# Expert rows of a mixture-of-experts block regrouped: 32 pair tiles of 2 x 48 rows become 24 tiles of 128 rows, with a merge product and eight gathers ahead

## The chip, the cores and the metric

The kernel runs on one core of one Trainium2 chip. The metric is the device time of that core in microseconds, lower is better. The kernel before took 1391.23 us (median of 3 runs).

## What is computed

The block is one transformer layer in float32 over 16 sequences of 256 tokens with 256 features (4096 tokens). Its first part is a decayed linear attention with 32 heads, then a residual and a layer norm without gains; the result is called x1. Its second part, which the change is about, is a mixture of experts on x1, then a residual and a layer norm again:

```python
scores = sigmoid(x @ gate_w)                       # 64 experts, 8 groups, the best 4 groups
topk_ids = top_k(masked scores + bias, 6)          # 6 experts a token
topk_w = scores[topk_ids] / sum * 2.5
order = argsort(flat expert of every (token, k))
pos = place within its expert
tok = order // K                                   # K = 6
valid = pos < CAP                                  # CAP = 2*(256*6//64) = 48
buf[expert, pos] = x[tok]                          # 64 experts x 48 rows of 256
h = silu(buf @ w_gate) * (buf @ w_up)              # 256 -> 96
out = h @ w_down                                   # 96 -> 256
y = segment_sum(out * topk_w, tok)                 # added to the token's row
y += silu(x @ ws_gate) * (x @ ws_up) @ ws_down     # shared expert, all tokens
```

So each of the 64 experts handles at most 48 rows, 3072 rows in all, and one token can stand under several experts.

## The kernel before, in words

The kernel is written by hand, engine by engine, with semaphores. Each engine runs its own program in order; SP issues the plain DMAs, POOL the indirect ones.

**Attention, us 0 to about 1200.** A loop over 16 sequences and 8 head groups (`sequences`, `step` on each engine). The router of the sequence before, the search for the tokens of each expert (`search`, `slots_*`) and the stores of x1 run in between. x1 with the 64 routing weights of each token behind it goes to `gather_rows` (4096 rows of 320 floats, 1280 bytes). The output sums lie in `sums`, two regions of 4096 rows of 256 floats.

**Tail of the attention, about 1200 to 1230.** No projections are left, and TensorE works on the shared expert, cut into 16 units (one of each sequence): `unit_gate_up` (g), `unit_down` (d), in the order of `TAIL`. Twelve units (`UNITS_AHEAD`) are done here; their elementwise products are POOL's (`unit_product`, L1486), the last of them before POOL's first gather. When the tokens of all experts are known (`ids`, 64 experts x 48), VectorE lays them out (L1381 to L1387), TensorE turns them into one column for each pair by a small product (L729 to L732), and VectorE writes the indices for the gathers and the slot numbers (L1389, L1390). Experts are taken in **pairs**: pair p has expert 2p in rows 0 to 47 and expert 2p+1 in rows 64 to 111 (`BANDS` = 112, `BAND` = 64; rows 48 to 63 stay unused). A scatter with addition must not hold the same row twice, so `find_doubles` (L1392 to L1403) compares the token numbers of both halves: SP writes them to memory (L473) and reads them back, broadcast (L475), and VectorE compares (L1396), reduces (L1398) and replaces the place of a doubled row (L1401, L1403).

**Loop over 32 pairs, about 1233 to 1336.** The order on TensorE in iteration p is written out (L791 to L803): `keep_busy` (L740, a product of 512 columns that nothing reads) and the two transposes of pair p+1 (`transpose_tokens`, L750), `gate_up(p)` (L761: 4 products of 192 columns, into partitions 0 to 47 and 64 to 111), `transpose_inner(p-1)` (L768, and L771, which puts the doubled rows of the second expert under the first's), `down(p-2)` (L778: 3 products of 256 columns). ScalarE evacuates the transposes (L1009), takes the SiLU (L1014) and evacuates the inner transpose (L1019). VectorE multiplies SiLU, weight and up-projection (L1419, two halves of 48 rows) and evacuates the result (`wo`, L1411, 4 buffers). In iterations 2, 8, 14 and 20 (`UP_AT`), and two later (`DOWN_AT`), TensorE also does one of the four units left.

POOL gathers 6 pairs ahead (`AHEAD`, 8 buffers), and for each pair p issues first gather p+6 (L1519), then scatter p (L1525). The scatter waits for `wo(p)`, and for the landing of scatter p-2:

```python
def scatter(p):
    pool.wait_ge(s_wo, p + 1)
    wait(pool, s_sc[p % 2], 16 * (p // 2))
```

SP loads the expert weights (576 KB for a pair, L454 and L455) into a ring of 16 pairs. The first 12 are loaded before the loop, and then one for each pair that is done:

```python
for p in range(FIRST_PAIRS, PAIRS):
    sp.wait_ge(s_md, p - FIRST_PAIRS + 1)
    load_pair(p, p % RING)
```

**End, about 1342 to 1385.** When all scatters have landed, SP reads both regions of `sums` in 16 pieces (L486), and VectorE, POOL and ScalarE add them, take the layer norm and store.

Of the kernel before, what the change touches and what calls it, by code (L numbers as in the profile page):

```python
# [15 lines left out]
F32 = mybir.dt.float32  # L16
F16 = mybir.dt.float16
U32 = mybir.dt.uint32
# [22 lines left out]
BANDS = 112  # L41
BAND = 64
# [5 lines left out]
AHEAD = 6  # L48
# [61 lines left out]
def block_kernel(nc, x, xT, wprep, normw, decay, eye, tri, w_router, bias2, w_shared, w_shared_down,  # L110
                 w_experts, w_down, slot_consts, dummy_rows, out):
# [9 lines left out]
    ids_t = nc.dram_tensor("slot_ids", (PAIRS, 2, CAP), F32, kind="Internal").ap()  # L121
# [3 lines left out]
    with ExitStack() as ctx:  # L125
# [3 lines left out]
        def sem(name):  # L129
# [86 lines left out]
        ids = sb("ids", [EXP, BAND])  # L216
        idsg = sb("idsg", [EXP, BAND])
        idss = sb("idss", [EXP, BAND])
        slotf = sb("slotf", [BANDS, PAIRS])
        twice = sb("twice", [BANDS, PAIRS])  # L220
        first = sb("first", [EXP, 1])
        slotc = sb("slotc", [EXP, 3 + PAIRS + BAND])
        dummies = sb("dummies", [P, PAIRS])
        pick, pairof, region, dummy = (slotc[:, 0:2], slotc[:, 2:2 + PAIRS], slotc[:, 2 + PAIRS:3 + PAIRS],
                                       slotc[:, 3 + PAIRS:3 + PAIRS + BAND])
        bandg = sb("bandg", [EXP, BANDS])
        bands = sb("bands", [EXP, BANDS])
        gidx = sb("gidx", [BANDS, PAIRS], U32)
        sidx = sb("sidx", [BANDS, PAIRS], U32)
# [9 lines left out]
        xg = carve(BANDS, XRING, ROW)  # L239
        wo = carve(BANDS, OUTBUF, HID)  # L240
        xgT = carve(P, 2, NC * BANDS).rearrange("p s (c n) -> p s c n", c=NC)
        mhs, mh, mhT = carve(BANDS, 2, FF), carve(BANDS, 2, FF), carve(FF, 2, BANDS + CAP)
# [21 lines left out]
        S1 = S[:, :, :].rearrange("p h n -> p (h n)")  # L264
        same = S1[0:BANDS, 0:PAIRS * CAP].rearrange("p (k n) -> p k n", k=PAIRS)

# [5 lines left out]
        pT, pH, pHT, pDn = [pA, pS[:, 0, :]], [pB, pS[:, 1, :]], [pC, pC], [pS[:, 2, :], pS[:, 3, :]]  # L272
# [55 lines left out]
        s_ring = [sem(f"s_ring{i}") for i in range(RING)]  # L328
# [6 lines left out]
        s_idr, s_idb, s_same, s_twice = sem("s_idr"), sem("s_idb"), sem("s_same"), sem("s_twice")  # L335
        s_sidx = sem("s_sidx")
# [12 lines left out]
        UP_AT = {2 + 6 * i: UNITS_AHEAD + i for i in range(SEQS - UNITS_AHEAD)}  # L349
# [33 lines left out]
        def _(sp):  # L383
# [10 lines left out]
            for i in range(PARTS):  # L394
# [8 lines left out]
                     (wsh, w_shared), (wsd[:, :], w_shared_down), (slotc[:, :], slot_consts), (dummies[:, :], dummy_rows)]  # L403
# [49 lines left out]
            def load_pair(p, r):  # L453
                sp.dma_start(ring[r][:, 0:4 * NC * FF], w_experts[p]).then_inc(s_ring[r], 16)  # L454
                sp.dma_start(ring[r][0:FF, 4 * NC * FF:PAIR_W], w_down[p]).then_inc(s_ring[r], 16)  # L455
# [27 lines left out]
            for i in range(2):  # L483
                sp.wait_ge(s_sc[i], 16 * (PAIRS // 2))
# [6 lines left out]
        def _(pe):  # L491
# [238 lines left out]
            for dst, a in ((pC, bandg), (pO, bands)):  # L730
                last = nc.tensor.matmul(dst[0:BANDS, 0:PAIRS], a[:, :], pairof, start=True, stop=True)
# [873 lines left out]
```

## Time and profile before

| | |
|---|---|
| median of 3 runs | 1391.23 us (1386.91 to 1393.55) |
| the profiled execution's own time | 1386.84 us |
| its span | 1385.0 us |
| busy TensorE | 1317.2 us (95%) |
| busy VectorE, ScalarE, POOL | 1178.0, 951.9, 457.1 us |
| attention and tail, to the first transpose of the pair loop | 0 to 1233.5 us |
| pair loop | 1233.5 to 1336.0 us |
| last scatter | issued at 1338.65, landed at about 1342.3 us |
| sums read, normed and stored | 1342.4 to 1385 us |

The time of the profiled execution is 1.84 us more than its span, which is what lies around the span. It stands 0.3% under the median and at the fast end of the three runs. Times in the rows below count from the start of the span.

### The profile page before, as it was taken

To read this page: it belongs to the slowest core of one execution; us is meant where nothing else is said; L and a number is where in the kernel's file an instruction comes from. 1 tells how busy PE (TensorE), PEld (TensorE's weight loads), DVE (VectorE), ACT (ScalarE), POOL (GpSimd) and SP (SyncE) were. 2 spreads that over 40 slices of the span, in tenths; PEclk is the share of its full clock that TensorE was granted. 3 is DMA by queue.
4 is the path that set the end of the run, shared out by engine and by line. 5 is a ranking of instruction groups with operands and counts; after the bars stand their busy time and mean duration, and the time that the engine had idled before them with its cause. 6 is when DMAs were issued, how large, how long until landed. Compare 5 with 4: busy or idle time off the path is not lost.

```text
span 1385.0 us, 39168 instructions
## 1 busy us (share of the span) xinstructions
PE 1317.2 (95%) x14971; PEld 1093.4 (79%) x14971; DVE 1178.0 (85%) x2393; ACT 951.9 (69%) x1735; POOL 457.1 (33%) x310
## 2 busy tenths in 40 slices
PE   7999999999999999999999999999999999889950
PEld 5888888888888888888888888888888888765530
DVE  7989899898989898999899898989898989653337
ACT  7777777777777777777777777777777777533315
POOL 0222322332323223232323233323223232447754
PEclk9999999999999999999999999999999999999985
DMA  8500000000000010100000000000010100879857
GB/s 315 203 2 17 27 17 26 17 27 17 26 17 26 9 34 1 38 5 17 26 17 26 17 26 17 26 17 26 9 34 9 34 1 22 270 233 257 220 117 298
DMA packets 53061, 88.00 MB, mean 64 GB/s; under 512 B 6752, under 2 KB 32192, under 8 KB 52032
## 3 DMA queue, kind: packets, MB, share of 16 engines
q1 hardware_dynamic: 41728, 70.33, 15.2%
q0 software_dynamic: 5632, 8.26, 3.4%
q10 hardware_dynamic: 5568, 7.34, 1.5%
q8 instruction: 119, 1.95, 0.6%
q14 instruction: 14, 0.11, 0.0%
HBM read 60.08 MB, written 25.83 MB: 62 GB/s over the span
## 4 chain that ended last, share of the span: by engine, by line
PE 89%; DMA 5%; DVE 2%; issue 2%; ACT 1%; POOL 1%; SPq 0%; ACTq 0%; DVEq 0%; POOLq 0%
PE pA L495 25%; PE pB L495 25%; PE pO L592 12%; PE pC L579 10%; PE pS L557 10%; DMA sums<-sb_stage,sb_sidx 2%; PE pC L495 2%; PE pS L778 1%; DMA sb_stage<-gather_rows,sb_gidx 1%; DMA sb_W<-sums 1%; PE pB L761 1%; PE pC L614 1%; PE pS L761 1%; PE pS L495 0%; SPq L486 0%
## 5 line engine op out<-in xcount | busy, mean ns | idle before, releaser
L1479 POOL TENSOR_TENSOR sb_acc<-sb_acc,sb_sq 128x512 f32<-128x512 f32 x112 | 246.1, 2197 | 681.8 <-ACT sb_sq L879 681.8
L495 PE MATMUL pB<-sb_xh,sb_W 128*128 128x256 f16 x2048 | 351.3, 274 | 0.5 <-ACT sb_kh L842 0.5
L495 PE MATMUL pB<-sb_xl,sb_W 128*128 128x256 f16 x1024 | 279.7, 273 | 0.0
L1095 DVE TENSOR_TENSOR sb_S<-pS,sb_D 128x1024 f32<-128x1024 f32 x250 | 231.6, 949 | 36.1 <-PE pS L557 35.4
L1101 DVE TENSOR_TENSOR sb_Shl<-sb_S,sb_Shl 128x1536 f16<-128x1536 f32 x122 | 220.1, 1804 | 2.3 <-ACT sb_Shl L868 2.0
L495 PEld LDWEIGHTS pB<-sb_xh,sb_W 128*128 128x128 f16 x2048 | 192.9, 99 | 32.8 <-DVE sb_W L1053 1.3
L868 ACT ACTIVATE sb_Shl<-sb_S 128x1024 f16<-128x1024 f32 x244 | 192.3, 835 | 12.2 <-DVE sb_S L1095 2.3
L495 PE MATMUL pA<-sb_xh,sb_W 128*128 128x256 f16 x1024 | 175.8, 274 | 5.6 <-DVE sb_W L1053 5.6
L495 PE MATMUL pA<-sb_W,sb_xh 128*128 128x256 f16 x1024 | 176.0, 274 | 2.2 <-ACT sb_qh L835 2.2
L592 PE MATMUL pO<-sb_Wo,sb_yh 128*128 128x256 f16 x1024 | 174.7, 273 | 1.5 <-DVE sb_yl L1074 1.5
L1074 DVE TENSOR_TENSOR sb_yl<-sb_y,sb_yh 128x512 f16<-128x512 f32 x128 | 161.4, 1261 | 2.1 <-ACT sb_yh L884 2.1
L579 PE MATMUL pC<-sb_Shl,sb_vh 128*64 128x128 f16 (+1 forms) x1952 | 144.1, 249 | 0.6 <-DVE sb_Shl L1101 0.6
L841 ACT ACTIVATE sb_k<-pB 128x512 f32<-128x512 f32 x128 | 76.5, 597 | 95.6 <-PE pB L495 95.6
L495 PE MATMUL pA<-sb_xl,sb_W 128*128 128x256 f16 x512 | 140.2, 274 | 0.0
L592 PE MATMUL pO<-sb_Wo,sb_yl 128*128 128x256 f16 x512 | 139.6, 273 | 0.0
L495 PE MATMUL pA<-sb_W,sb_xl 128*128 128x256 f16 x512 | 139.6, 273 | 0.0
L834 ACT ACTIVATE sb_q<-pA 128x512 f32<-128x512 f32 x128 | 76.4, 597 | 84.7 <-PE pA L495 84.7
L557 PE MATMUL pS<-sb_qh,sb_kl 64*128 64x256 f16 (+1 forms) x1024 | 126.0, 243 | 0.0
L874 ACT ACTIVATE sb_gt<-pB 128x512 f32<-128x512 f32 x128 | 76.4, 597 | 68.4 <-PE pB L495 66.4
L579 PEld LDWEIGHTS pC<-sb_Shl,sb_vh 128*64 128x64 f16 x1952 | 102.2, 110 | 26.2 <-issue 25.4
L579 PE MATMUL pC<-sb_Shl,sb_vl 128*64 128x256 f16 x976 | 121.0, 246 | 0.0
L557 PE MATMUL pS<-sb_qh,sb_kh 64*128 64x256 f16 (+1 forms) x1024 | 120.7, 245 | 0.0
(223 smaller groups left out, 2698.4 us busy)
## 6 DMA issues: line engine op xcount, KB each, us to landing
sb_stage<-wprep SPq DMA_DIRECT2D x7, 1280.0 KB, 6.3
sb_W<-sums SPq DMA_DIRECT2D x16, 512.0 KB, 11.4
sb_W<-w_experts SPq DMA_DIRECT2D x16, 384.0 KB, 5.8
gather_rows<-sb_xr SPq DMA_DIRECT2D x16, 320.0 KB, 2.3
sb_D<-w_experts SPq DMA_DIRECT2D x12, 384.0 KB, 4.0
sb_xs<-xT SPq DMA_DIRECT2D x17, 256.0 KB, 2.9
sb_D<-decay SPq DMA_DIRECT2D x8, 512.0 KB, 7.3
sb_xn<-x SPq DMA_DIRECT2D x16, 256.0 KB, 3.0
```

Source lines behind the costliest of these rows:

```text
L495: last = nc.tensor.matmul(dst, a, m, start=(i == 0), stop=(i == len(terms) - 1), **kw)
L557: last = nc.tensor.matmul(pS[:, 2 * u + e, at:at + T - q0], k[lo:hi, u, k0:k0 + P], x_[lo:hi, u, q0:T], start=(n == 0), stop=(n == len(pro ...
L579: last = nc.tensor.matmul(pC[64 * e:64 * e + 64, u * T + t * P:(u + 1) * T], v[:, t, head * HD:(head + 1) * HD], s[:, head, a:z_], start=( ...
L592: last = nc.tensor.matmul(pO[:, t * HID:(t + 1) * HID], (yh, yl)[y][:, u * T + t * P:u * T + (t + 1) * P], Wo[:, w, q, u * HID:(u + 1) * H ...
L834: nc.scalar.activation(q32[:, :, :], bank, ACT.Silu, scale=1 / W_SCALE)
L841: nc.scalar.activation(k32[:, :, :], bank, ACT.Silu, scale=1 / W_SCALE)
L868: nc.scalar.activation(Sh[:, :, a:z_], S[:, :, a:z_], ACT.Copy).then_inc(s_Sh, 1)
L874: nc.scalar.activation(gt[q % 2][:, :], pB[:, :], ACT.Tanh, scale=0.5 / W_SCALE).then_inc(s_ge, 1)
L1074: nc.vector.tensor_tensor(yl[:, :], y32[:, :], yh[:, :], ALU.subtract).then_inc(s_yl, 1)
L1095: nc.vector.tensor_tensor(scores_at(h)[:, :, a:z_], pS[:, :, a:z_], d[:, :, 0:z_ - a], ALU.mult).then_inc(s_Sm, 1)
L1101: nc.vector.tensor_tensor(Sl[:, :, :], S[:, :, :], Sh[:, :, :], ALU.subtract).then_inc(s_Sl, 1)
L1479: nc.gpsimd.tensor_tensor(acc[:, :], acc[:, :], sq[:, :], ALU.add).then_inc(s_acc, 1)
```

## The change

The 48 slots of each expert are split into a main block of 32 rows (`BLOCK`) and a rest of 16 (`REST`). Eight experts fill three tiles of 128 rows: two tiles ("kinds" 0 and 1) hold the main blocks of four experts each, the third (kind 2) the rests of all eight. 64 experts make 24 tiles without gaps. For each block of 32 rows the product takes its own expert's weights and writes its own 32 output partitions; in a tile of kind 2 a block has rows of two experts, and its products run twice, with the other expert's 16 columns held at zero.

A token can stand in up to 4 (or 8) experts of one tile. `equal` (128 x 128) says which rows of a tile have the same token. It is multiplied with an upper triangle, and a last product (`merge`) adds to each row the rows of the same token before it; the rows that have a later one of the same token are sent to a dummy place, and only the last is scattered to the token. So the routing weight is applied before the merge, by ScalarE (`weighted`), and no longer in the product of SiLU and up-projection.

Eight gathers run ahead in place of six. The weight ring is released in groups of four pairs (three tiles). The last two products of the units ahead move from POOL to VectorE. The eight products that cleared the output banks (L788) go.

```diff
-    BANDS = 112
-    BAND = 64
+    TILES = EXP * CAP // P
+    KINDS = 3
+    BLOCK = 32
+    REST = CAP - BLOCK
-    AHEAD = 6
+    AHEAD = 8
+    EQS, EQB = 8, 4
+def experts_of(t):
+    g, kind = t // KINDS, t % KINDS
+    if kind < 2:
+        return [[8 * g + 4 * kind + j] for j in range(4)]
+    return [[8 * g + 2 * j, 8 * g + 2 * j + 1] for j in range(4)]
...
-        UP_AT = {2 + 6 * i: UNITS_AHEAD + i for i in range(SEQS - UNITS_AHEAD)}
+        UP_AT = {2 + 5 * i: UNITS_AHEAD + i for i in range(SEQS - UNITS_AHEAD)}
...
-            sp.dma_start(ids_t.rearrange("k e n -> (k e) n"), idss[:, 0:CAP]).then_inc(s_idr, 16)
-            sp.wait_ge(s_idr, 16)
-            sp.dma_start(same[BAND:BANDS, :, :], ids_t[:, 0, :].unsqueeze(0).broadcast_to([CAP, PAIRS, CAP])).then_inc(s_idb, 16)
+            sp.dma_start(ids_main, ids[:, 0:BLOCK]).then_inc(s_idr, 16)
+            sp.dma_start(ids_rest, ids[:, BLOCK:CAP]).then_inc(s_idr, 16)
+            sp.wait_ge(s_idr, 32)
+            n = EXP // 8 // 2
+            for i in range(2):
+                rows = id_rows[i].rearrange("p (g n) -> p g n", g=n)
+                for src, at, z_ in ((ids_main, 0, 2 * P), (ids_rest, 2 * P, KINDS * P)):
+                    src = src[i * EXP // 2:(i + 1) * EXP // 2, :].rearrange("(g e) n -> g (e n)", g=n)
+                    sp.dma_start(rows[:, :, at:z_], src.unsqueeze(0).broadcast_to([P, n, z_ - at])).then_inc(s_idb[i], 16)
             sp.wait_ge(s_D, STEPS)
             for p in range(FIRST_PAIRS, PAIRS):
-                sp.wait_ge(s_md, p - FIRST_PAIRS + 1)
+                sp.wait_ge(s_md, p - FIRST_PAIRS + 1 if p < RING else KINDS * ((p - RING) // 4 + 1))
                 load_pair(p, p % RING)
...
+            def gate_up(t):
+                blocks = experts_of(t)
+                pe.wait_ge(s_xgT, t + 1)
+                g = t // KINDS
+                pe.wait_ge(s_ring[g % (RING // 4)], 4 * 32 * (g // (RING // 4) + 1))
+                wait(pe, s_mh, t - 1)
+                parts = len(blocks[0])
+                for c in range(NC):
+                    for h in range(parts):
+                        for j, b in enumerate(blocks):
+                            at = slice(BLOCK * j, BLOCK * (j + 1))
+                            last = nc.tensor.matmul(pH[t % 2][at, 0:2 * FF], xgT[:, t % KINDS + h, c, at],
+                                                    ring_gu[b[h] // 2 % RING][:, b[h] % 2, c, :],
+                                                    start=(c == 0 and h == 0), stop=(c == NC - 1 and h == parts - 1))
                 last.then_inc(s_mgu, 1)
+            def transpose_inner(t):
+                pe.wait_ge(s_mh, t + 1)
+                wait(pe, s_mhT, t)
+                nc.tensor.transpose(pHT[0:FF, 0:P], mh[:, t % 2, :], ident[:, :]).then_inc(s_mht, 1)
+            def down(t):
+                pe.wait_ge(s_mhT, t + 1)
+                wait(pe, s_ysb, t)
+                for h in range(parts):
+                    for j, b in enumerate(blocks):
+                        at = slice(BLOCK * j, BLOCK * (j + 1))
+                        last = nc.tensor.matmul(pDn[at, 0:HID], mhT[t % KINDS + h][:, at], ring_d[b[h] // 2 % RING][:, b[h] % 2, :],
+                                                start=(h == 0), stop=(h == parts - 1))
                 last.then_inc(s_md, 1)
+            def merge(t):
+                pe.wait_ge(s_ysb, t + 1)
+                pe.wait_ge(s_eq, t + 1)
+                wait(pe, s_wo, t)
+                nc.tensor.matmul(pM[:, 0:HID], equal[t % EQS], ysb[t % 2], start=True, stop=True).then_inc(s_mm, 1)
...
-            for bank in pH + pDn:
-                nc.tensor.matmul(bank[0:BANDS, 0:HID], zeros[:, 0:BANDS], zeros[:, 0:HID], start=True, stop=True)
             transpose_tokens(0)
+            for p in range(TILES + 3):
+                if p + 1 < TILES:
                     transpose_tokens(p + 1)
+                if p < TILES:
                     gate_up(p)
+                if 1 <= p <= TILES:
                     transpose_inner(p - 1)
+                if 2 <= p <= TILES + 1:
                     down(p - 2)
+                if p >= 3:
+                    merge(p - 3)
...
+                if kind < 2:
+                    last = nc.scalar.activation(mhT[kind], pHT[0:FF, 0:P], ACT.Copy)
+                else:
+                    for h in range(2):
+                        to, at = [a.rearrange("p (j h n) -> p j h n", j=4, h=2)[:, :, h, :] for a in (mhT[kind + h], pHT[0:FF, 0:P])]
+                        last = nc.scalar.activation(to, at, ACT.Copy)
...
+            def weighted(t):
+                act.wait_ge(s_md, t + 1)
+                wait(act, s_mm, t - 1)
+                nc.scalar.activation(ysb[t % 2], pDn[:, 0:HID], ACT.Copy, scale=weight[:, t:t + 1]).then_inc(s_ysb, 1)
...
+            for dst, at, z_, n, pick in ((cand_main, 0, BLOCK, 4, pick_main), (cand_rest, BLOCK, CAP, 8, pick_rest)):
+                shape = [EXP, n, z_ - at]
+                last = nc.vector.tensor_tensor(dst[:, :].rearrange("e (l s) -> e l s", l=n), ids[:, at:z_].unsqueeze(1).broadcast_to(shape),
+                                               pick.unsqueeze(2).broadcast_to(shape), ALU.mult)
+            nc.vector.tensor_copy(slotf[:, :], pC[:, 0:TILES])
+            chain.link(nc.vector.tensor_scalar(gathf[:, :], pC[:, 0:TILES], float(TOK - 1), None, ALU.min))
+            chain.ready()
+            nc.vector.tensor_copy(gidx[:, :], gathf[:, :]).then_inc(s_idx, 1)
+            chain.link(nc.vector.tensor_tensor(slotr[:, :], slotf[:, :], region_less, ALU.add))
+            for j in (UNITS_AHEAD - 2, UNITS_AHEAD - 1):
+                unit_product(j)
+            def find_equals(n):
+                a, z_ = n * EQB, (n + 1) * EQB
+                dve.wait_ge(s_idb[a * P // half_rows], 32)
+                wait(dve, s_mm, z_ - EQS)
+                for t in range(a, z_):
+                    rows = id_rows[t * P // half_rows][:, t * P % half_rows:t * P % half_rows + P]
+                    nc.vector.scalar_tensor_tensor(equal[t % EQS], rows, slotf[:, t:t + 1], triu[:, 0:P], ALU.is_equal, ALU.mult,
+                                                   accum_out=count_eq[:, t:t + 1]).then_inc(s_eq, 1)
+                dve.wait_ge(s_eq, z_)
+                nc.vector.scalar_tensor_tensor(place[:, a:z_], count_eq[:, a:z_], FAR, slotr[:, a:z_], ALU.mult, ALU.add).then_inc(s_place, 1)
+                dve.wait_ge(s_place, 2 * n + 1)
+                nc.vector.tensor_tensor(placed[:, a:z_], place[:, a:z_], dummy[:, a:z_], ALU.min).then_inc(s_place, 1)
+                dve.wait_ge(s_place, 2 * n + 2)
+                nc.vector.tensor_copy(sidx[:, a:z_], placed[:, a:z_]).then_inc(s_sidx, 1)
+            find_equals(0)
+            def evacuate(t):
+                dve.wait_ge(s_mm, t + 1)
+                if t >= OUTBUF:
+                    dve.wait_ge(s_sc[t % 2], 16 * (t // 2 + 1 - OUTBUF // 2))
+                nc.vector.tensor_copy(wo[:, t % OUTBUF, :], pM[:, 0:HID]).then_inc(s_wo, 1)
+            for p in range(TILES + 3):
+                if p < TILES:
                     dve.wait_ge(s_mhs, p + 1)
                     wait(dve, s_mht, p - 1)
+                    nc.vector.scalar_tensor_tensor(weights8[:, p % 2, :], xg[:, p % XRING, at:at + 8], 1.0, onehot[:, p % KINDS, :],
+                                                   ALU.mult, ALU.mult, accum_out=weight[:, p:p + 1])
+                    nc.vector.tensor_tensor(mh[:, p % 2, :], mhs[:, p % 2, :], pH[p % 2][:, FF:2 * FF], ALU.mult).then_inc(s_mh, 1)
+                if p >= 3:
+                    evacuate(p - 3)
+                if p % EQB == EQB - 1 and p + 1 < TILES:
+                    find_equals(p // EQB + 1)
...
             def scatter(p):
+                pool.wait_ge(s_sidx, p // EQB + 1)
                 pool.wait_ge(s_wo, p + 1)
...
+            for p in range(TILES):
+                if p + AHEAD < TILES:
                     gather(p + AHEAD)
                 scatter(p)
```

## Rows read from the trace of the kernel before

**Rows 1.** The page: the span, and TensorE's busy time.
```profile
span 1385.0 us, 39168 instructions
...
PE 1317.2 (95%) x14971; PEld 1093.4 (79%) x14971; DVE 1178.0 (85%) x2393; ACT 951.9 (69%) x1735; POOL 457.1 (33%) x310
```

**Rows 2.** Windows: stretch, us, busy PE, PEld, DVE, ACT, POOL, clock, DMA, GB/s.
```profile
1237.00:1336.00 99.00, 97.79 (x689) 55.66 (x687) 35.04 (x101) 32.29 (x105) 69.22 (x57) 1.00 0.81 194
```

**Rows 3.** Timeline of TensorE, one iteration (start us, length us, instruction).
```profile
1254.85 0.39 PE L740 MATMUL pA<-sb_x1hl,sb_wshh 128*128 128x512 f16 x1
1255.08 0.36 PE L750 MATMUL pA<-sb_ident,sb_stage 112*128 112x112 f32 x2
1255.36 0.86 PE L761 MATMUL pS<-sb_W,sb_stage 128*48 128x192 f32 x8
1256.15 0.30 PE L768 MATMUL pC<-sb_ident,sb_stage 112*96 112x112 f32 x1
1256.38 0.36 PE L771 MATMUL pC<-sb_S,sb_stage 48*96 48x48 f32 x2
1256.68 1.06 PE L778 MATMUL pS<-sb_W,sb_stage 96*48 96x256 f32 x6
1257.67 0.39 PE L740 MATMUL pS<-sb_x1hl,sb_wshh 128*128 128x512 f16 x1
```

**Rows 4.** Timeline of TensorE: the down-projection of a unit, and what follows it.
```profile
1248.24 1.14 PE L495 MATMUL pO<-sb_wsd,sb_q 96*128 96x256 f32 x4
1249.21 0.38 PE L740 MATMUL pA<-sb_x1hl,sb_wshh 128*128 128x512 f16 x1
```

**Rows 5.** Timeline of TensorE from 1255.3 to 1255.6 us: instructions begun by then.
```profile
1255.36 0.53 PE L761 MATMUL pS<-sb_W,sb_stage 128*48 128x192 f32 x4
```

**Rows 6.** Timeline of TensorE: first and last row of a unit's gate and up.
```profile
1241.26 0.31 PE L495 MATMUL pO<-sb_W,sb_wshh 128*96 128x256 f16 x1
...
1242.60 0.38 PE L740 MATMUL pA<-sb_x1hl,sb_wshh 128*128 128x512 f16 x1
```

**Rows 7.** Timelines of VectorE, POOL, SP, TensorE at the loop's start; idle in brackets.
```profile
1233.32 1.75 DVE L1396 TENSOR_TENSOR sb_S<-sb_S,sb_slotf 48x1536 f32<-48x1536 f32 x1 [7.02 <-DMA sb_S<-slot_ids]
...
1229.09 1.19 POOL L1519 DMA_INDIRECT sb_stage<-gather_rows,sb_gidx  x1 [0.19 <-issue]
...
1228.76 0.35 SPq L475 DMA_DIRECT2D sb_S<-slot_ids  x1
...
1235.47 0.41 PE L750 MATMUL pS<-sb_ident,sb_stage 112*128 112x112 f32 x2 [1.32 <-DMA sb_stage<-gather_rows,sb_gidx]
...
1237.90 0.30 PE L768 MATMUL pC<-sb_ident,sb_stage 112*96 112x112 f32 x1
```

**Rows 8.** Timeline of POOL late in the loop: scatter, gather, scatter.
```profile
1313.00 1.49 POOL L1525 DMA_INDIRECT sums<-sb_stage,sb_sidx  x1 [0.30 <-issue]
1314.79 0.95 POOL L1519 DMA_INDIRECT sb_stage<-gather_rows,sb_gidx  x1 [0.30 <-issue]
1316.04 1.48 POOL L1525 DMA_INDIRECT sums<-sb_stage,sb_sidx  x1 [0.30 <-issue]
```

**Rows 9.** DMA queues and a scatter's landing, 1250 to 1275 us.
```profile
q1 hardware_dynamic: 1953, 4.53, 58.5%
q0 software_dynamic: 1287, 1.94, 41.3%
...
sums<-sb_stage,sb_sidx POOLq DMA_INDIRECT x8, 5.8
```

**Rows 10.** Groups of instructions and timeline of VectorE: evacuation; weighted copy with a sum.
```profile
L1411 DVE COPY sb_stage<-pS 112x256 f32<-112x256 f32 x32 | 13.6, 424 | 19.1 <-PE pS L778 19.1
...
1217.59 0.22 DVE L1212 SCALAR_TENSOR_TENSOR sb_wsel<-sb_mask,sb_sc 128x64 f32<-128x64 f16 x1
```

**Rows 11.** Timelines of TensorE and POOL: the last of the pair loop.
```profile
1334.11 1.93 PE L778 MATMUL pS<-sb_Wo,sb_stage 96*48 96x256 f32 x12
...
1338.65 1.45 POOL L1525 DMA_INDIRECT sums<-sb_stage,sb_sidx  x1 [0.63 <-issue]
```

More of the change, by code:

```diff
@@ L262, in block_kernel @@
         late_sh = [a.rearrange("p (k n) -> p k n", k=FIN) for a in late_sh]
-        S1 = S[:, :, :].rearrange("p h n -> p (h n)")
-        same = S1[0:BANDS, 0:PAIRS * CAP].rearrange("p (k n) -> p k n", k=PAIRS)
+        half_rows = TILES // 2 * P
+        id_rows = [a.rearrange("p h n -> p (h n)")[:, 0:half_rows] for a in (S[:, :, :], whole_S[1])]
         CHUNK = REGIONS * FIN * HID
@@ L327, in block_kernel @@
         s_slots = sem("s_slots")
-        s_ring = [sem(f"s_ring{i}") for i in range(RING)]
+        s_ring = [sem(f"s_ring{i}") for i in range(RING // 4)]
         s_gath = [sem(f"s_gath{i}") for i in range(XRING)]
@@ L334, in block_kernel @@
         s_sc = [sem(f"s_sc{i}") for i in range(2)]
[L335 to L336 removed]
+        s_idr, s_idb = sem("s_idr"), [sem(f"s_idb{i}") for i in range(2)]
+        s_eq, s_place, s_sidx = sem("s_eq"), sem("s_place"), sem("s_sidx")
+        s_ysb, s_mm = sem("s_ysb"), sem("s_mm")
         s_fl = [sem(f"s_fl{i}") for i in range(FINALS)]
@@ L729, in _ @@
             pe.wait_ge(s_ids, 1)
-            for dst, a in ((pC, bandg), (pO, bands)):
-                last = nc.tensor.matmul(dst[0:BANDS, 0:PAIRS], a[:, :], pairof, start=True, stop=True)
-            last.then_inc(s_idp, 1)
+            nc.tensor.matmul(pC[:, 0:TILES], cand_main[:, :], tile_main, start=True, stop=False)
+            nc.tensor.matmul(pC[:, 0:TILES], cand_rest[:, :], tile_rest, start=False, stop=True).then_inc(s_idp, 1)
             for u in "g11 d10 d11".split():
@@ new lines, in inner, with evacuate_inner @@
+            def inner(t):
+                act.wait_ge(s_mgu, t + 1)
+                wait(act, s_mh, t - 1)
+                nc.scalar.activation(mhs[:, t % 2, :], pH[t % 2][:, 0:FF], ACT.Silu).then_inc(s_mhs, 1)
+            def evacuate_inner(t):
+                act.wait_ge(s_mht, t + 1)
+                wait(act, s_md, t + 1 - KINDS)
+                kind = t % KINDS
+                if kind < 2:
+                    last = nc.scalar.activation(mhT[kind], pHT[0:FF, 0:P], ACT.Copy)
+                else:
+                    for h in range(2):
+                        to, at = [a.rearrange("p (j h n) -> p j h n", j=4, h=2)[:, :, h, :] for a in (mhT[kind + h], pHT[0:FF, 0:P])]
+                        last = nc.scalar.activation(to, at, ACT.Copy)
+                last.then_inc(s_mhT, 1)
@@ L1506, in step @@
                 if last_b and q == 3:
-                    for j in range(4, UNITS_AHEAD):
+                    for j in range(4, UNITS_AHEAD - 2):
                         unit_product(j)
@@ L1536, in _ @@
                 pool.wait_ge(done, 16 * len(range(i, UNITS_AHEAD, UEV)))
-            for p in range(PAIRS):
-                if p + AHEAD < PAIRS:
+            for p in range(TILES):
+                if p + AHEAD < TILES:
                     gather(p + AHEAD)
@@ L1595 @@
         "slot_consts": slot_consts,
-        "dummy_rows": (REGIONS * TOK + P * (pair % REGIONS)[None, :] + np.arange(P)[:, None]).astype(np.float32),
+        "row_consts": row_consts,
     }
```

194 lines of the change are left out of this document (73 added, 121 removed).

## The prediction

> **What bounds the kernel now.** I read the page first: TensorE is busy for 95% of the span [rows 1], but the change touches only the last 150 us, so its worth has to be read there. The windows view of the pair loop shows TensorE busy 97.8 of 99 us at the full granted clock, POOL 69 us, VectorE 35, ScalarE 32, and the DMA engines 81% [rows 2]. So the loop is bound by TensorE, with POOL and the DMAs not far behind. The timeline of TensorE splits one iteration into its groups; I take the step from the start of one group to the start of the next [rows 3]: idle filler 0.23, two transposes 0.28, gate and up 0.79, inner transpose 0.23, product for doubled rows 0.30, down 0.99; together 2.82 us. 32 pairs take 90.2 us. The four units in the loop take 1.34 us for gate and up [rows 6] and 0.97 for down [rows 4], 2.31 each, 9.2 in all. The sum, 99.4 us, stands against the 100.5 us from the transpose at 1235.47 [rows 7] to the last product's end at 1336.04 [rows 11]: the model holds.
>
> **Prices of matrix work.** The gate and up products are 8 instructions of 192 columns (a float32 product is two instructions). By 1255.6, 0.24 us after the first began, four had begun [rows 5]: two column groups run side by side, and 8 instructions are 4 rounds. A unit's down-projection runs its 4 instructions of 256 columns one after another: 0.97 us [rows 4]. L778 takes 0.99 for 6 instructions [rows 3]: two rounds of two and two of one, also 4 rounds. From 0.99 (4 rounds of 256) and 0.79 (4 rounds of 192, worth 3 of 256) a round of 256 costs 0.20, one of 192 costs 0.15, and each group has a head of 0.19.
>
> **The loop after the change, part by part.** The new products are in four blocks of 32 partitions. The trace shows two groups side by side, not four; I take it that four run as two do, since the second one costs nothing visible. One after another in twos is the other end, below.
> - Filler and transposes: 112 rows become 128, 0.23 + 0.31.
> - Gate and up, kinds 0 and 1: 8 products, 16 instructions, 4 rounds, 0.79. Kind 2: 32 instructions, 8 rounds, 0.19 + 1.20 = 1.39.
> - Inner transpose 0.24. The product L771 goes (0.30).
> - Down: kinds 0 and 1 two rounds, 0.59; kind 2 four rounds, 0.99.
> - Merge: one full product of 256 columns, two instructions: 0.19 + 0.40 = 0.59.
>
> So a tile of kind 0 or 1 takes 2.75 and one of kind 2 takes 3.75; three take 9.25, and 24 take 74.0 in place of 90.2. With the units' 9.2, unchanged, TensorE's loop is 83.2 us: **16.2 less**.
>
> **The start.** Before, POOL's first gather waits behind the last unit product and starts at 1229.09; TensorE's second transpose waits for the second gather until 1235.47, and VectorE stands 7.02 us until the slot numbers land at 1233.32, so that the first inner transpose starts only at 1237.90 [rows 7]. After: two products leave POOL's queue for VectorE's, which is idle there anyway; they delay only what stands behind them there, the equality, and it waits for a DMA. The first gather can go some 2 us earlier, an estimate that matters little, since the equality ends later than the gathers; and two gathers more cost POOL 2.5 us [rows 8] before its first scatter, at a time when it waits for the first result. The eight clearing products lie where TensorE waits for a gather: worth nothing. On VectorE the next thing late is the equality. The read-back grows from 0.29 to 1.57 MB (128 partitions x 3072 x 4 bytes) in four DMAs; the small one took 4.5 us from 1228.76 [rows 7]. It starts some 0.7 us earlier, and only its first half is needed first: I take the same landing, 1233, with 1232 and 1237 as ends. Then VectorE does 4 comparisons of 128 x 128 (two 64-wide instructions of the kind of 0.22 each with their reads of the sum [rows 10], 0.4) and three small steps, 2.4 us, until 1235.4; before, its work on the doubled rows lasted until shortly before 1237.90. With the first product of SiLU and up-projection, and the step to TensorE, the first inner product follows at 1236.4: **1.5 less**, from 2.5 less to 2.5 more.
>
> **VectorE and ScalarE in the loop.** VectorE: 0.3 weight, 0.3 product, 0.42 evacuation [rows 10], 0.6 for its share of comparisons: 1.6 us a tile. ScalarE gets a fourth evacuation, 1.3 to 1.7. Both lie under a tile's 2.75 to 3.75. But comparisons come in blocks of 2.4 us every fourth iteration, ahead of the next product in VectorE's queue. That product is wanted by TensorE one iteration later, after filler, transposes and gate-up; by my steps it is ready some 0.4 us before. I cost this at nothing; if a comparison takes 0.6 and not 0.4, five blocks lose about 0.4 us each, 2 us.
>
> **POOL and the DMAs.** One scatter and one gather with their gaps take 3.04 us [rows 8], almost all of 2.82. Rows go from 112 to 128: a scatter is 1.48 to 1.69 us, a gather 0.95 to 1.09, by a fixed cost or by rows. A tile is 3.03 to 3.38 us of POOL against TensorE's mean (83.2 / 24) of 3.47. So POOL stays just under. The DMAs: weights cost 58.5% of 25 us for 4.53 MB, 1.9 us of all engines a pair; tokens 41.3% of 25 us for 1.94 MB, 5.3 us a MB [rows 9]. Token traffic falls from 8.26 MB (32 x 112 rows of 1280 and 1024 bytes) to 7.08, but a tile is 0.295 MB, 1.6 us. The releases in groups of four bring all 20 pairs (38 us) into the first 13 tiles: 4.5 us of demand a tile against 3.47. The weights can be late, eight tiles lie between their issue and their use. The scatters cannot: scatter p waits for p-2. At 5.8 us [rows 9] and 0.8 to the next start, two scatters need 6.6 us before; with 128 rows 7.4, or 3.7 a tile over some 12 tiles, against 3.47: 2.8 us, most of it taken up by the four buffers. I put 2 us on the last scatter's distance behind TensorE.
>
> **The sum.** TensorE has done 2.97 us of its 83.2 before the first inner transpose (three pairs of transposes, two fillers, two gate-ups), so it ends at 1236.4 + 80.2 = 1316.6. The last scatter stood 2.6 us behind the end at 1336.04 [rows 11]; now 4.6, with 0.5 for its size: 1321.7 in place of 1338.65, **17 us less**. What follows is unchanged. On the profiled execution's 1386.84 that is 1369.8. It lies 4.4 us under the median, so the forecast for the median is 1391.23 - 17 = **1374**.
>
> **Rivals.**
> - **Two blocks at a time (slower).** If only two column groups run together, gate and up take 16 rounds of 0.15 more for three tiles and down 8 of 0.20: 4.0 us, 32 in all. TensorE ends at 1348.6, the last scatter at 1351.7: 13 us more, **1404**. It decides where a round of four costs more than 1.5 rounds of two (17 of 32). Against it: the second group started with no visible delay [rows 5]. For it: no row shows four, nor four streams of float32 read at once. Chance 0.12.
> - **Four blocks at a loss.** With rounds of four a quarter dearer, 24 rounds for three tiles (16 x 0.15 + 8 x 0.20 = 4.0) cost 1.0 more, 8 in all: **1382**. Chance 0.10. The Trainium skill ("TensorE: Matmul & The Clock Gate", Part 3, Packing small matmuls) gives 2.38 times for three column tiles of 32, that is 0.79 of the ideal; by that rule it would be this case, and the trace, whose two groups lose almost nothing, doesn't bear it out.
> - **Scatters set the pace.** With all weights pressed into the first 13 tiles a scatter takes 8.5 us to land (5.8 now): 4.6 us a tile to tile 14, from a first scatter at 1244 (1236.4 and two iterations and a unit's gate-up on) to 1309, then 2.5 a tile as the weights are in: 1331. The gain shrinks to 8: **1383**. For it: the DMA engines are full in that stretch already. Against: token packets and weight packets share them now and the lag stays small. Chance 0.10.
> - **A late read-back** of 1.57 MB shifts all by 3 or 4 us: **1378**. Chance 0.08, inside the range.
>
> **How the numbers follow.** The base case, with its own spread 1366 to 1380, has 0.56; the late read-back 0.08; the two at 1382 and 1383 have 0.20; two at a time 0.12; 0.04 for other things. The range 1364 to 1390 leaves out the slow rival and both tails, 0.2. A measurement of this kernel can tell about 0.5%, 7 us, from no change: faster than 1384.3 gets 0.77 (base, read-back, two thirds of the middle cases), within 0.5% 0.11, slower than 1398 0.12.
>
> **What the changed profile would show.** Timeline of a kind 0 tile: L761's successor with 16 instructions in about 0.8 us, the merge 0.6, three tiles in 9.3 us. The loop would end at about 1317 and the last scatter start near 1321. A gate and up of 1.4 us in kinds 0 and 1 would be the first rival; idle TensorE before merges or gathers with scatters over 8 us the third; a first comparison later than 1235 the fourth.

## The result: 0.6% faster

The changed kernel takes 1378.21 us (median of 5 runs, 1376.7 to 1383.0), the kernel before 1390.62 (5 runs). The ratio is 0.9939, with a 95% interval of 0.9916 to 0.9963: 8.5 us less, where 17 were forecast. The two medians lie 12.4 us apart, a little outside that interval. The five runs of the kernel before spread over nearly 8 us, and its three later sets of 17 runs have medians of 1386.6 to 1387.8, which is nearer to the ratio; so the text goes by ratios. The time lies within the forecast's range. The profiled executions took 1380.61 and 1386.84 us.

The page of the changed kernel:

```profile
span 1378.8 us, 39739 instructions
...
PE 1305.0 (95%) x15235; PEld 1085.5 (79%) x15235; DVE 1168.2 (85%) x2455; ACT 956.6 (69%) x1751; POOL 439.3 (32%) x292
...
q0 software_dynamic: 4608, 7.08, 2.6%
```

The packing does on TensorE what it was to do. A whole iteration with kind 0 or 1 (columns as in [rows 3]):

```profile
1243.76 0.38 PE L770 MATMUL pA<-sb_x1hl,sb_wshh 128*128 128x512 f16 x1
1243.98 0.38 PE L780 MATMUL pA<-sb_ident,sb_stage 128*128 128x128 f32 x2
1244.29 0.86 PE L794 MATMUL pS<-sb_W,sb_stage 128*32 128x192 f32 x16
1245.08 0.31 PE L802 MATMUL pC<-sb_ident,sb_stage 128*96 128x128 f32 x1
1245.32 0.64 PE L812 MATMUL pS<-sb_W,sb_qh 96*32 96x256 f32 x8
1245.89 0.70 PE L820 MATMUL pS<-sb_ql,sb_kh 128*128 128x256 f32 x2
1246.43 0.38 PE L770 MATMUL pS<-sb_x1hl,sb_wshh 128*128 128x512 f16 x1
```

Its gate and up has 16 instructions (L794) where [rows 3] has 8, in the same 0.79 us, and eight of them have begun by 1244.5, where [rows 5] had four:

```profile
1244.29 0.53 PE L794 MATMUL pS<-sb_W,sb_stage 128*32 128x192 f32 x8
```

Four blocks of 32 columns run as two of 48 did. The loop as a whole does not keep that pace. Windows of the changed kernel (columns: stretch, length, busy PE, PEld, DVE, ACT, POOL, clock, DMA share, GB/s):

```profile
1232.00:1240.00 8.00, 4.96 (x41) 2.35 (x41) 2.12 (x15) 1.58 (x7) 2.96 (x4) 0.57 0.84 307
1240.00:1272.00 32.00, 32.00 (x395) 19.18 (x396) 10.65 (x62) 15.03 (x50) 16.04 (x13) 1.00 0.84 224
1272.00:1284.00 12.00, 9.12 (x73) 5.10 (x66) 3.12 (x19) 2.40 (x8) 5.71 (x5) 0.72 1.07 291
1284.00:1294.00 10.00, 10.00 (x121) 5.74 (x119) 2.29 (x12) 5.11 (x17) 5.16 (x4) 1.00 1.01 299
1294.00:1304.00 10.00, 8.04 (x70) 3.85 (x72) 2.77 (x16) 1.91 (x7) 6.62 (x5) 0.67 0.76 192
1304.00:1326.00 22.00, 22.00 (x265) 12.40 (x261) 7.26 (x40) 9.96 (x34) 14.19 (x11) 0.99 0.46 66
```

There are three holes in TensorE's work, at 1232, 1274 and 1294 us, each with a clock under 1.00 behind it (the granted clock as a share of the full one; 0.50 is its lower level). The timeline of TensorE says what ended them (idle before the instruction in brackets):

```profile
1235.04 0.69 PE L780 MATMUL pS<-sb_ident,sb_stage 128*128 128x128 f32 x2 [3.11 <-DMA sb_stage<-gather_rows,sb_gidx]
...
1277.30 0.69 PE L780 MATMUL pS<-sb_ident,sb_stage 128*128 128x128 f32 x2 [2.88 <-DMA sb_stage<-gather_rows,sb_gidx]
...
1296.34 0.44 PE L780 MATMUL pS<-sb_ident,sb_stage 128*128 128x128 f32 x2 [1.96 <-DMA sb_stage<-gather_rows,sb_gidx]
```

All three wait for gathered rows. The chain of waits leads from there to scatters that take 9 to 10 us to land, against a median of 5.8 [rows 9], and to a gather that takes 7.6 (start us, us until the landing):

```profile
1255.13 10.43 DMA sums<-sb_stage,sb_sidx
...
1266.38 9.91 DMA sums<-sb_stage,sb_sidx
...
1277.11 8.92 DMA sums<-sb_stage,sb_sidx
...
1288.75 7.55 DMA sb_stage<-gather_rows,sb_gidx
```

The next gather stands behind the waiting scatter in POOL's queue:

```profile
1266.38 1.59 POOL L1594 DMA_INDIRECT sums<-sb_stage,sb_sidx  x1 [5.16 <-DMA sums<-sb_stage,sb_sidx]
```

In the same stretch SP sends the expert weights of twelve pairs, in two blocks of eight and four; the last four pairs follow from 1286.75, ahead of the third hole. Its timeline, first and last of the two blocks:

```profile
1254.15 0.44 SPq L479 DMA_DIRECT2D sb_W<-w_experts  x1
...
1263.71 0.43 SPq L479 DMA_DIRECT2D sb_W<-w_experts  x1
...
1270.32 0.34 SPq L479 DMA_DIRECT2D sb_D<-w_experts  x1
...
1273.86 0.43 SPq L479 DMA_DIRECT2D sb_D<-w_experts  x1
```

The last scatter starts at 1333.42, 5.2 us before that of [rows 11]:

```profile
1333.42 1.55 POOL L1594 DMA_INDIRECT sums<-sb_stage,sb_sidx  x1 [0.30 <-issue]
```

### The profile page after: what moved, and what is told of

It is laid out like the page before. It is cut to its first block, busy times and chain, and to the rows that moved or that the text cites. A ratio compares the mean times of both kernels' runs of the same rounds, so it can differ in the third digit from the quotient of the medians.

```text
span 1378.8 us, 39739 instructions
## 1 busy us (share of the span) xinstructions
PE 1305.0 (95%) x15235; PEld 1085.5 (79%) x15235; DVE 1168.2 (85%) x2455; ACT 956.6 (69%) x1751; POOL 439.3 (32%) x292
## 4 chain that ended last, share of the span: by engine, by line
PE 88%; DMA 6%; DVE 2%; issue 2%; ACT 1%; POOL 0%; SPq 0%; ACTq 0%; DVEq 0%; POOLq 0%
PE pA L526 25%; PE pB L526 24%; PE pO L623 12%; PE pC L610 10%; PE pS L588 10%; DMA sums<-sb_stage,sb_sidx 3%; PE pC L526 2%; DMA sb_stage<-gather_rows,sb_gidx 1%; DMA sb_W<-sums 1%; DMA sb_stage<-wprep 1%; PE pS L812 1%; PE pS L794 1%; PE pB L794 1%; PE pS L820 1%; PE pC L645 1%
```

## Experiments

Each ratio is to the kernel before, timed on the same chip; the changed kernel has 0.9939.

**1. Weights one by one.** The same loads, released evenly:

```diff
-                sp.wait_ge(s_md, p - FIRST_PAIRS + 1 if p < RING else KINDS * ((p - RING) // 4 + 1))
+                sp.wait_ge(s_md, max(1 + (p - FIRST_PAIRS) * 4 // 5, 0 if p < RING else KINDS * ((p - RING) // 4 + 1)))
```

> The changed kernel with the expert weights of pairs 12 to 31 released one by one, 0.8 tiles apart (after 1, 1, 2, 3, 4, 5, 5, 6, 7 ... 16 tiles done), in place of bursts. Burst theory: in the changed kernel 12 pairs' loads go out between 1253 and 1275 and scatters take about 10 us to land; paced, they land in 6 to 7 us as before the change, the two later waits of TensorE for a gather (2.9 and 2.0 us) go, and with them the half clock behind them (about 6 us); POOL's last scatter starts near 1322, 9 to 12 us earlier: 1366 to 1370, ratio to the kernel before 0.983 to 0.987. Volume theory: the DMA engines have the same bytes to move in any order, so scatters stay at 9 to 10 us: 1376 to 1380, ratio 0.993. If the size of a scatter (128 rows) is what makes it slow: same, also where no weights are loaded.

Measured: 1374.09 us, ratio 0.9893 (0.9874 to 0.9913). The two later waits of TensorE are gone, and the clock stays up:

```profile
1231.00:1244.00 13.00, 6.73 (x44) 2.99 (x45) 2.35 (x17) 2.47 (x8) 7.88 (x9) 0.61 0.85 264
1244.00:1322.00 78.00, 77.34 (x931) 45.00 (x930) 26.73 (x148) 34.00 (x117) 48.26 (x36) 1.00 0.86 220
```

The loop from the first inner transpose (1242.82) to the last product's end (1322.61) takes 79.8 us, where my sum had 80.2. In the changed kernel it takes 90.7 (1239.48 to 1330.15). The gain is less than expected (1366 to 1370 us). Of the profiled execution, 1375.07 us, 3.3 us of that are a later start of the loop: its first gather waited until 1230.04 for the landing of the last stored token rows. For the other five executions this isn't shown. The volume theory falls: with as many bytes, or more, moved in 1255 to 1300 (13.08 MB against 12.82) TensorE no longer waits. Scatters still reach past two turns of POOL, with up to 2.4 us of waiting for one, against 5.2:

```profile
1289.17 1.59 POOL L1594 DMA_INDIRECT sums<-sb_stage,sb_sidx  x1 [0.30 <-issue]
...
1297.62 1.59 POOL L1594 DMA_INDIRECT sums<-sb_stage,sb_sidx  x1 [2.37 <-DMA sums<-sb_stage,sb_sidx]
```

The scatter of 1297.62 waited for that of 1289.17. With the 0.8 us that lie between a landing and the next start in these traces, the earlier one took about 7.7 us to land, an estimate; two more worked out in the same way took 6.7 and 7.1. That is under the 9 to 10 of the bursts and over the expected 6 to 7.

**2. The kernel before, with bursts.**

```diff
-                sp.wait_ge(s_md, p - FIRST_PAIRS + 1)
+                sp.wait_ge(s_md, p - FIRST_PAIRS + 1 if p < RING else 4 * ((p - RING) // 4 + 1))
```

> The kernel before, with nothing of the change but the weight ring released in groups of four pairs (pairs 16 to 31 wait for 4, 8, 12, 16 pairs done). Burst theory: scatters behind a burst take 8 to 10 us to land, POOL falls back by some 2 us a burst, gathers come late and TensorE waits: 2 to 8 us slower than before, ratio 1.002 to 1.006. Volume theory: the same bytes, ratio 1.000 within 0.2%. The 32 pairs give each burst 11 us where three tiles give it 9, so less than the changed kernel loses.

Measured: 1396.52 us, ratio 1.0062 (1.0041 to 1.0083), at the upper end of the burst theory's 1.006. The chain has two landings as long as those of the changed kernel, and TensorE waits for gathers five times in the loop, the longest of them:

```profile
1253.19 9.36 DMA sums<-sb_stage,sb_sidx
...
1285.18 9.59 DMA sums<-sb_stage,sb_sidx
```

```profile
1307.40 0.41 PE L750 MATMUL pS<-sb_ident,sb_stage 112*128 112x112 f32 x2 [2.66 <-DMA sb_stage<-gather_rows,sb_gidx]
```

So the grouped release costs time by itself, and with 112-row scatters too: their size is not what makes them slow.

**3. Half of the read-back later.**

```diff
             for i in range(2):
+                if i == 1:
+                    sp.wait_ge(s_mgu, 1)
                 rows = id_rows[i].rearrange("p (g n) -> p g n", g=n)
```

> The changed kernel with the second half of the token numbers' read-back (0.79 of 1.57 MB, for tiles 12 to 23) sent only after the first gate and up. Start theory: the read-back fills all DMA engines from 1229 to 1237 and so makes the second gather land at 1235.0, 7.9 us after its issue, and TensorE idle for 3.1 us and then slow at half clock for some 4 us (2 us lost); with half of it gone the second gather lands by 1233 and the start is 2 to 4 us earlier: ratio 0.990 to 0.992. Rival: the start's gain is eaten by the scatters' pace behind it, which the weights set: ratio 0.993 as the changed kernel, with the first inner transpose at 1237 and not 1239.5 all the same.

Measured: 1377.23 us, ratio 0.993 (0.9904 to 0.9955), no difference from the changed kernel, and the rival's number. TensorE has the second gather 0.6 us earlier; measured from the gather's own issue (1227.95, against 1227.08) the time falls from 7.96 to 6.46 us:

```profile
1234.41 0.69 PE L782 MATMUL pS<-sb_ident,sb_stage 128*128 128x128 f32 x2 [0.64 <-DMA sb_stage<-gather_rows,sb_gidx]
...
1276.70 0.44 PE L782 MATMUL pS<-sb_ident,sb_stage 128*128 128x128 f32 x2 [2.06 <-DMA sb_stage<-gather_rows,sb_gidx]
```

The first inner transpose came at 1238.87, against 1239.48, and not at 1237 as the rival said. The later waits stay. One pair of executions would not carry the difference, but the others agree: with the whole read-back, in the profiles of the changed kernel and of experiments 1, 4, 5 and 11, TensorE has the second gather 6.8 to 8.3 us after its issue; with the late half, here and in experiments 9 and 10, after 6.2 to 6.7.

**4. Six gathers ahead.** `AHEAD = 6` in the changed kernel.

> The changed kernel with six gathers ahead in place of eight. If the two more gathers cover late scatters: TensorE waits for gathers more often and longer, 3 to 10 us slower than the changed kernel, ratio 0.996 to 1.001. If they only press more on the DMA engines at the start: up to 1 us faster, ratio 0.992 to 0.994.

Measured: 1391.04 us, ratio 1.0028 (1.0012 to 1.0043), past the upper end of the first theory (1.001). Packing and merge with six gathers ahead are slower than the kernel before. TensorE waits for gathers at seven places; behind the start, the timeline has among others

```profile
1260.94 0.69 PE L780 MATMUL pA<-sb_ident,sb_stage 128*128 128x128 f32 x2 [2.64 <-DMA sb_stage<-gather_rows,sb_gidx]
...
1292.88 0.44 PE L780 MATMUL pA<-sb_ident,sb_stage 128*128 128x128 f32 x2 [3.20 <-DMA sb_stage<-gather_rows,sb_gidx]
...
1308.05 0.44 PE L780 MATMUL pS<-sb_ident,sb_stage 128*128 128x128 f32 x2 [3.42 <-DMA sb_stage<-gather_rows,sb_gidx]
```

**5. Weights one by one and six ahead.** Edits 1 and 4.

> The changed kernel with paced weights and six gathers ahead. With bursts, six ahead in place of eight cost 0.9% (1.0028 against 0.9939), since a gather stands behind a scatter that waits for a landing. If eight ahead only made good what the bursts did, paced weights make six enough: 0.989 to 0.991. If the lead is wanted in itself (a gather lands 4 to 7 us after its issue, and TensorE is quicker through a tile than before): 0.992 to 0.996.

Measured: 1384.78 us, ratio 0.9973 (0.9955 to 0.9991). The lead is worth 0.8% here and 0.9% with bursts: it has worth as such, and somewhat more than the second case of the expectation had.

**6. Eight ahead in the kernel before.** `AHEAD = 8` there, nothing else.

> The kernel before with eight gathers ahead in place of six, nothing else. It tells how much of the change's gain is the packing and how much the lead. In the kernel before TensorE waits for gathers for some 1 us in the loop behind the start, and two more gathers delay the first scatter by at most 2.5 us: ratio 0.998 to 1.001. If the lead is worth as much there as in the changed kernel (0.8 to 0.9%): 0.991 to 0.993, and the packing gives next to nothing by itself.

Measured: 1386.75 us, ratio 1.0002 (0.9984 to 1.0019). So the lead is worth nothing without the packing; and with six ahead the packing is worth nothing with bursts (1.0028) and 0.3% with paced weights (0.9973). In the kernel before, gather p+6 goes out behind scatter p-1, whose rows come from `down` two iterations on; in the changed one the merge adds a third, and so takes one iteration off the lead. That this iteration is what the two gathers replace is my reading of the code; the runs show only that six are enough in one kernel and not in the other.

**7. Both improvements.** Edits 1 and 3.

> The changed kernel with both edits: weights of pairs 12 to 31 released one by one, 0.8 tiles apart, and the second half of the read-back sent after the first gate and up. The late half alone moved nothing while the bursts stood (0.993), the paced weights alone gave 0.9893. If the start is a loss of its own that the bursts only covered, the second gather lands 2 us earlier and, with no later waits, the end comes 1.5 to 3 us earlier than with the paced weights alone: ratio 0.987 to 0.988. Rival: scatters set the pace from the first on, so that an earlier start of TensorE only makes it wait later: 0.989 to 0.990.

Measured: 1371.03 us, ratio 0.9866 (0.984 to 0.9892), just under the expected 0.987 to 0.988: clearly faster than the changed kernel and than the kernel before. It is 3 us under edit 1 alone, with intervals that overlap, so what the late half adds is likely and not shown. One wait of TensorE for a gather (0.74 us) is left in the loop; its loop, 1241.16 to 1321.82, takes 80.7 us.

**8. Filler products for the first waits.** Edit 7, and

```diff
+            for _ in range(14):
+                keep_busy(0)
             transpose_tokens(0)
+            for _ in range(12):
+                keep_busy(1)
             for p in range(TILES + 3):
```

> As the kernel with paced weights and the late half, and with 14 filler products of 512 columns ahead of the first token transpose and 12 ahead of the first gate and up (in the place of TensorE's waits for the first two gathers; the change had taken eight clearing products from there). Clock theory: the idle 3 to 6 us there cost TensorE its clock (granted 0.50 at 1235 to 1238), which makes the first tiles' some 4 us of work take 2 us longer; filled, the granted clock stays 1.00 and the end comes 1 to 2 us earlier: 0.0010 off the ratio. Rival: the fillers (26 x 0.215 = 5.6 us) are longer than the waits and push the first transposes back by as much as the clock gives: no change within 0.1%.

Measured: 1370.88 us, ratio 0.9869 (0.9843 to 0.9895): no difference. The clock does what it was to do. Windows of edit 7 first, then of this one:

```profile
1235.00:1238.00 3.00, 2.40 (x17) 1.16 (x21) 1.67 (x11) 0.77 (x2) 2.36 (x3) 0.50 0.76 285
```

```profile
1235.00:1238.00 3.00, 3.00 (x29) 1.48 (x26) 0.50 (x2) 0.00 (x0) 1.49 (x2) 1.00 0.75 187
```

But it gives nothing at the end of the kernel. The timeline says where it goes:

```profile
1233.54 2.97 PE L772 MATMUL pS<-sb_x1hl,sb_wshh 128*128 128x512 f16 x13
1236.35 0.38 PE L782 MATMUL pS<-sb_ident,sb_stage 128*128 128x128 f32 x2
```

The second token transposes stand behind the fillers, with no wait for the gather. That one was issued at 1228.11; with the 6.2 to 6.7 us of the other kernels with a late half it was there at 1234.3 to 1234.8, an estimate, so the fillers cost 1.5 to 2 us, about as much as the first tiles gain by the clock. That fits the rival. It is not shown more closely: the profiled executions of edit 7 and of this one start their first gather 1.8 us apart. Fewer fillers, or the kernel before's eight clearing products in the place where they stood, were not tried.

**9. The first free ring places filled sooner.** Edit 7, and

```diff
-                sp.wait_ge(s_md, max(1 + (p - FIRST_PAIRS) * 4 // 5, 0 if p < RING else KINDS * ((p - RING) // 4 + 1)))
+                sp.wait_ge(s_mgu, p - FIRST_PAIRS + 1) if p < RING else sp.wait_ge(s_md, max(3 + (p - RING) * 4 // 5, KINDS * ((p - RING) // 4 + 1)))
```

> As the kernel with paced weights and the late half, but pairs 12 to 15 (whose ring places are free from the start) released after 1, 2, 3, 4 gate-ups, two tiles sooner than by done tiles, and pairs 16 to 31 from 3 tiles done on, 0.8 tiles apart and not before their place is free: 3, 3, 4, 5, 6 ... 15. The DMA engines stand at 0.66 between 1237 and 1260 in the changed kernel and are full behind it. If what is left of the scatters' lag comes from the full stretch, using the empty one takes 1 to 2 us off: ratio 0.986 to 0.987. Rival: weights do more harm under the first scatters and gathers than later: 0.989.

Measured: 1371.2 us, ratio 0.9873 (0.9848 to 0.9898). No difference from edit 7, and the interval leaves room for both theories. TensorE has no wait for a gather left in its loop.

**10. Ten ahead of the scatters**, on edit 7 (`AHEAD = 10`, still 8 buffers).

> Paced weights, late half of the read-back, and POOL's gathers issued ten tiles ahead of the scatters (still 8 buffers: gather q waits for the product of tile q-8, which is done before scatter q-10 can go, so it costs no wait, and only takes the gather from behind two scatters). Gather theory: eight ahead is worth 0.8% over six even with paced weights, so the lead has worth as such; with eight the trace has one wait left (0.7 us) and some runs of it more; ten take them off: 0.985 to 0.986. Rival: with eight ahead the loop is bound by TensorE and the chain of scatters behind it, and ten gives nothing: 0.9866.

Measured: 1371.02 us, ratio 0.9877 (0.9853 to 0.9901): no difference from edit 7 beyond the interval, as the rival says. Eight are enough once the weights are paced.

**11. Ten ahead, with bursts.** `AHEAD = 10` in the changed kernel.

> The changed kernel, weights in bursts, with gathers ten tiles ahead of the scatters. If the bursts do their harm by way of the gathers that stand behind a late scatter (TensorE idle 2.9 and 2.0 us, then at half clock), ten ahead give back what the paced weights gave: 0.988 to 0.990. If they do it by the scatters' own landing (10 us for two, and four result buffers), ten change little: 0.993, and TensorE waits for a free result buffer in place of a gather.

Measured: 1378.77 us, ratio 0.9925 (0.9902 to 0.9949), as the changed kernel. The waits have changed their name; beside the two shown there is a third of 1.32 us. TensorE's timeline:

```profile
1278.94 0.67 PE L820 MATMUL pS<-sb_ql,sb_kh 128*128 128x256 f32 x2 [1.97 <-DVE sb_stage L1480]
1290.13 0.67 PE L820 MATMUL pS<-sb_ql,sb_kh 128*128 128x256 f32 x2 [3.43 <-DVE sb_stage L1480]
```

and the waits view, for VectorE behind it:

```profile
DVE sb_stage L1480 <- DMA sums<-sb_stage,sb_sidx: 14.0, 4, 5.8
```

TensorE now waits for the merge's bank, which VectorE can't empty, since the result buffers still hold rows whose scatters (9 to 11 us) have not landed. So the bursts do their harm through the scatters' landing, and the late gathers of the changed kernel are only where it shows first. Whether more result buffers would take the waits off was not tried.

**12. Unit products back on POOL**, ahead of its gathers.

```diff
-            for j in (UNITS_AHEAD - 2, UNITS_AHEAD - 1):
-                unit_product(j)
...
-                    for j in range(4, UNITS_AHEAD - 2):
+                    for j in range(4, UNITS_AHEAD):
```

> The changed kernel with the products of units 10 and 11 back on POOL, ahead of its first gather. The first gather goes out at about 1228 and not at 1225.5. If the start is set by the second gather's landing (7.9 us after its issue, behind the read-back): all tiles come up to 2.5 us later, ratio 0.994 to 0.9957. If it is set by the read-back and the comparisons of tokens, as I had predicted: no change, 0.9939.

Measured: 1380.24 us, ratio 0.9941 (0.9919 to 0.9964). The first gather goes out at 1228.81, 3.3 us after that of the changed kernel, and the ratio shows no loss. The medians are 2 us apart, against kernels before of 1386.57 and 1390.62; a loss of 2 us is within the interval. In the profiled execution, the slowest of its six, the later gather does go through: the first inner transpose starts at 1242.18 and the last scatter at 1336.56, 2.7 and 3.1 us after those of the changed kernel. So the profiles speak for the first theory and the times decide nothing. That part is open.

## Why the prediction was half right

- **The time** is 4.2 us over the forecast, the profiled execution 10.8 (1380.61 against 1369.8). The smaller number is luck: the forecast was moved up by 4.4 us because the profiled execution before lay that far under its median, and this one's lies 2.4 over. That 1378 is also the number of the rival "A late read-back" is chance, since the read-back was not late. The mechanism was right on TensorE and wrong on the DMAs and the start.
- **TensorE's work** was right, term by term. Kind 0 and 1: 2.67 us (forecast 2.75). Down 0.57 (0.59), merge 0.54 (0.59), transposes 0.31, inner transpose 0.24. Kind 2's gate and up 1.44 (1.39). From the first inner transpose to the end: 79.8 us with the weights paced (80.2).
- **Four blocks at once** held, in full: a group of four starts and ends as a group of two did. The two rivals on it fall, the one at a quarter's loss too. By the Trainium skill ("TensorE: Matmul & The Clock Gate", Part 3, Packing small matmuls) three column tiles give 2.38 times; here four blocks of 192 columns in float32 take the time that two took, and the measurement decides.
- **POOL's prices** were within their bounds: a scatter of 128 rows 1.59 us, in the middle (1.48 to 1.69 forecast), a gather 0.99, near the low end (0.95 to 1.09).
- **The DMA step failed**: "The weights can be late, eight tiles lie between their issue and their use. The scatters cannot", and then "2.8 us, most of it taken up by the four buffers. I put 2 us". I saw that the loads were pressed together and priced a scatter behind them by its median before, 5.8 us scaled to 6.6 for 128 rows. It took 9 to 10. The third rival, "Scatters set the pace", had the mechanism, 8.5 us, and 1383; the measured 1378 lies between it and the base case. The cost is 10.5 us in the loop (90.7 against 80.2), of which 4.8 are idle at two gathers, and nearly all the rest is work behind them at half the clock. Experiments 1, 2 and 11 show the cause.
- **The start** was forecast 1.5 us earlier and is 1.6 later (first inner transpose at 1239.48, [rows 7] has 1237.90), 3.1 us off. I looked for a late read-back, and that landed as forecast:

```profile
1233.32 0.37 DVE L1465 SCALAR_TENSOR_TENSOR sb_kh<-sb_S,sb_slotf,sb_triu 128x128 f32<-128x128 f32 x1 [6.19 <-DMA sb_S<-slot_ids_rest]
```

  Two steps failed. The first is "the equality ends later than the gathers": the comparisons were through at 1235.1, and the second gather landed at 1235.0, 7.9 us after its issue, with TensorE's transposes and two gate-ups still to come behind it, 2.4 us of work by the forecast's prices. That makes 1.1 us of the 3.1. Experiment 3 shows that the read-back, which the change made larger, has a part in that landing; with half of it gone 6.5 us are left, against 4.9 in the kernel before, and that rest stays open.
- **"Worth nothing"**, said of the eight clearing products, is the second, and makes the other 2 us. The work from the second transposes to the first inner transpose took 4.4 us here and 2.4 before, and the clock is why. Timeline and window of the kernel before, then the window of the changed one:

```profile
1230.87 0.66 PE L788 MATMUL pB<-sb_zeros 128*112 128x256 f32 x2 [0.78 <-ACT sb_gt L896]
1231.36 1.46 PE L788 MATMUL pS<-sb_zeros 128*112 128x256 f32 x6
...
1231.00:1237.00 6.00, 3.97 (x24) 2.36 (x24) 3.61 (x3) 0.96 (x3) 4.78 (x5) 1.00 0.80 217
```

```profile
1231.00:1237.00 6.00, 2.58 (x21) 1.15 (x21) 1.69 (x11) 0.77 (x2) 3.65 (x4) 0.63 1.00 357
```

  Before, the clearing products lay between waits of 0.78 and 0.70 us, and the clock stayed at 1.00. Here two waits of about 3 us follow each other, and the first two tiles run at half clock and take almost twice their time. The sum had no term for the clock. Experiment 8 shows that products in this place keep it up. How much of its fall comes from the missing products and how much from the later gather is not shown.
- **The end**: the last scatter started 3.3 us behind TensorE's end (4.6 forecast), and from its start to the span's end there are 45.4 us (46.3 before).
- The ledger: forecast last scatter 1321.2, plus 3.1 (start), plus 10.5 (loop), less 1.3 (lag) gives 1333.5; measured 1333.42. (The forecast's last scatter, 1321.7, has 0.5 us more for its own size.) The ledger sorts the miss; it is no proof of its terms, since they are read from the same trace.
- **"Two gathers more"** I had costed as harmless and worth nothing. They are worth 0.9% with bursts and 0.8% with paced weights: without them the change as it was made is a loss (1.0028). The sum had no term for how far gathers run ahead. The merge makes each scatter, and so the gather behind it, one iteration later; that this is the reason is argued from the code (experiment 6).

## What to carry to other kernels

When an engine gets faster, look at what is queued behind what it now waits for: the packing saved 16 us on TensorE (from the second token transposes to the last product 84.3 us in experiment 1, 100.6 before), and two numbers beside it, how far gathers run ahead and how evenly the weights are released, decided between 0.3% slower and 1.1% faster. Release prefetches one by one, not by groups, when a chain of small transfers that wait for each other's landing shares the DMA engines; price such a transfer by its landing under the worst burst. A longer lead did not help where the wait was for the landing itself (experiment 11): it only moved the place where it shows. When a change takes idle-time work away from an engine, look at the clock behind it.

## What the runs showed of the hardware

- Four column blocks of 32 run at once in float32, each with its own moving operand: 32 instructions of 192 columns in 1.44 us, 16 in 0.79.
- Behind a wait of 2.88 us the granted clock stood at its lower level (0.50), and stayed there for some six microseconds of dense work, from 1277.30 on; behind the wait of 1.96 us at 1296.34 it fell too:

```profile
1277.00:1282.00 5.00, 4.70 (x31) 2.18 (x32) 1.73 (x14) 1.44 (x5) 4.27 (x3) 0.50 1.05 278
1282.00:1285.00 3.00, 3.00 (x27) 2.60 (x29) 0.48 (x2) 0.74 (x4) 0.99 (x1) 0.70 1.08 273
```

- A scatter of 128 rows landed in 9 to 10 us while the loads of a burst were under way, and in 3.8 us at the end of the loop (3.77 and 3.84 in the chain), when no loads were under way.
- Sixteen more rows cost POOL little: 112 to 128 rows took a scatter from 1.48 to 1.59 us and a gather from 0.95 to 0.99, about half of proportional, or less.
